# Sine stage of a two-layer transformer kernel: ScalarE writes the whole turns, VectorE makes the sine's argument from PSUM

## What is computed

```python
x = x + ffn(layernorm(x), W1, b1, theta, w_real, w_imag, W2, b2)
# ffn:
hidden = x @ W1 + b1                       # 256 -> 1024
imag   = w_imag * sin(theta + hidden * 0.1)
phase  = cos(theta) * w_real + sin(theta) * w_imag
act    = relu(hidden + phase * imag * 0.1)
out    = act @ W2 + b2                     # 1024 -> 256
```

## Time and profile before

| what | value |
|---|---|
| three runs | 991.68, 993.87, 995.29 us |
| median | 993.87 us |
| the profiled execution | 987.04 us |
| its span, first to last instruction | 985.2 us |
| granted TensorE clock, mean over the span | 0.986 of full |
| sine stage in the span | about 256 to 474.5 us |

### The profile page before, as it was taken

The page is one execution under the profiler, slowest core; times in us unless marked ns, Lnnn a source line. Parts: engine busy times, 40 slices in busy tenths (PEclk is TensorE's granted clock), DMA queues, the critical chain, the costliest instruction groups (busy, mean ns, idle before and its releaser), DMA issues. The chain is left out here.

```text
span 985.2 us, 20329 instructions
## 1 busy us (share of the span) xinstructions
PE 912.7 (93%) x7332; PEld 806.9 (82%) x7332; DVE 830.7 (84%) x2172; ACT 485.3 (49%) x1019; POOL 465.8 (47%) x663
## 2 busy tenths in 40 slices
PE   6999999999589999999799999999987999999996
PEld 4889998898478888888689889898876888888885
DVE  5799999997499999998588888899868889889874
ACT  2453443433188787788244333343454444544442
POOL 2233334331266666664322332433247777777662
PEclk9799999999799999999999999999999999999999
DMA  9020000000000000000100000000000000000000
GB/s 341 34 98 2 2 2 1 2 3 1 1 1 1 1 1 1 1 1 1 53 2 2 2 2 2 1 2 2 1 1 1 22 23 1 22 23 22 23 22 22
DMA packets 6083, 18.32 MB, mean 19 GB/s; under 512 B 864, under 2 KB 2784, under 8 KB 5472
## 3 DMA queue, kind: packets, MB, share of 16 engines
q1 hardware_dynamic: 5264, 16.52, 4.4%
q10 hardware_dynamic: 720, 0.50, 0.2%
HBM read 12.83 MB, written 4.19 MB: 17 GB/s over the span
## 5 line engine op out<-in xcount | busy, mean ns | idle before, releaser
L868 PE MATMUL a_psO<-vblk,a_prob 128*128 128x51 f32 (+1 forms) x1280 | 150.0, 273 | 0.0
L868 PEld LDWEIGHTS a_psO<-vblk,a_prob 128*128 128x128 f32 x1280 | 149.6, 194 | 0.0
L1513 PE MATMUL f_psGU<-wgu,f_xTs 128*128 128x512 f32 (+1 forms) x576 | 138.5, 385 | 3.1 <-ACT f_silu L1463 3.1
L507 DVE TENSOR_REDUCE a_mx<-a_psS 128x4 f32<-128x308 f32 x256 | 115.1, 470 | 17.4 <-PE a_psS L784 15.8
L704 ACT COPY a_xTs<-a_psQ 128x256 f32<-128x256 f32 x64 | 23.8, 372 | 206.8 <-PE a_psQ L793 206.8
L715 ACT ACTIVATE a_prob<-a_psT 128x512 f32<-128x512 f32 (+1 forms) x192 | 101.0, 526 | 40.8 <-PE a_psT L840 39.3
L1513 PEld LDWEIGHTS f_psGU<-wgu,f_xTs 128*128 128x128 f32 x576 | 101.9, 189 | 17.7 <-DVE f_xTs L1258 3.4
L840 PE MATMUL a_psT<-ident,a_shifted 128*128 128x128 f32 x640 | 106.3, 281 | 10.8 <-ACT a_prob L715 7.9
L515 DVE TENSOR_TENSOR a_shifted<-a_psS,a_mx 128x308 f32<-128x308 f32 x256 | 114.6, 469 | 0.0
L1095 PEld LDWEIGHTS s_psY<-w,s_hid 128*128 128x128 f32 x768 | 99.4, 188 | 16.6 <-POOL s_hid L1013 12.2
L1095 PE MATMUL s_psY<-w,s_hid 128*128 128x256 f32 x768 | 104.0, 284 | 5.6 <-POOL s_hid L1013 4.9
(11 more groups left out here) (157 smaller groups left out, 1912.8 us busy)
## 6 DMA issues: line engine op xcount, KB each, us to landing
out_x<-x SPq DMA_DIRECT2D x8, 512.0 KB, 2.6
x<-in_x SPq DMA_DIRECT2D x3, 1024.0 KB, 12.8
w<-in_w SPq DMA_DIRECT2D x1, 2304.0 KB, 9.1
w<-in_w SPq DMA_DIRECT2D x2, 1024.0 KB, 17.6
a_mask<-in_mask SPq DMA_DIRECT2D x4, 308.0 KB, 4.0
wat<-in_att SPq DMA_DIRECT2D x1, 1024.0 KB, 22.4
x<-in_x SPq DMA_DIRECT2D x1, 768.0 KB, 9.5
wat<-in_att SPq DMA_DIRECT2D x2, 256.0 KB, 5.5
```

Of the source, the lines that this page charges most:

```text
L507: nc.vector.tensor_reduce(mx[:, u, j * BH:(j + 1) * BH], psS[j][:, 0:BH * KV].rearrange("p (h k) -> p h k", k=KV), AX.X, ALU.max).then_inc ...
L868: mm = nc.tensor.matmul(psO[:, CH[c] * VW:(CH[c] + n) * VW], prob[:, v, c * P:(c + 1) * P], vblk[:, t // R, c * NJ * VW:(c * NJ + n) * VW] ...
L1513: mm = nc.tensor.matmul(psGU[:, n0:n1], xTs[:, u, a, k * P:(k + 1) * P], wgu[:, b, k, n0:n1], start=(n == 0), stop=(n == len(TERMS) - 1))
```

## The change

ScalarE's pass over PSUM now writes the rounded number of turns: the output tile `turn` is int32, so the conversion rounds. VectorE then makes the argument in one `scalar_tensor_tensor` (psH + phase - turns) that reads psH from PSUM and the turns from SBUF, in place of two instructions. For this, psH must already be in turns: the first weight matrix is multiplied by TURNS = 0.1 / 2 pi when it is split, the coefficient is scaled likewise, and the two Relu passes scale back. `turn` has four buffers and `arg` two. The waits follow; `turn_set` falls away.

```diff
--- before.py
+++ after.py
@@ -37,6 +37,7 @@
 MAGIC = 1.5 * 2.0 ** 23
 TWO_PI = 6.283185307179586
 PI_IN = 3.1415925
+TURNS = 0.1 / TWO_PI
 MASKED = -1e20
 
 ATT_FIRST, ATT_LAST, ATT_LOOP_FROM, ATT_LOOP_TO = -3, T + 2, 5, T - 3
@@ -335,7 +336,7 @@
         self.link(dve, nc.vector.tensor_tensor(cs, ang[:, 3, 8:16], cols[:, C_WR:C_WR + 8], ALU.mult))
         self.link(dve, nc.vector.tensor_tensor(sn, ang[:, 3, 0:8], cols[:, C_WI:C_WI + 8], ALU.mult))
         self.link(dve, nc.vector.tensor_tensor(sn, sn, cs, ALU.add))
-        self.link(dve, nc.vector.scalar_tensor_tensor(self.g["coef"][:], sn, 0.1, cols[:, C_WI:C_WI + 8], ALU.mult,
+        self.link(dve, nc.vector.scalar_tensor_tensor(self.g["coef"][:], sn, 0.1 * TURNS, cols[:, C_WI:C_WI + 8], ALU.mult,
                                                       ALU.mult))
         self.link(dve, nc.vector.tensor_scalar(thb[:], thb[:], 1.0 / TWO_PI, None, ALU.mult))
 
@@ -344,14 +345,21 @@
 
     src, high, _ = w_quarter(g, n)
     act.wait_ge(g["in_ffn"], 32)
-    nc.scalar.copy(high, src).then_inc(g["w_high"], 1)
+    if n < 2:
+        nc.scalar.activation(high, src, ACT.Copy, scale=TURNS).then_inc(g["w_high"], 1)
+    else:
+        nc.scalar.copy(high, src).then_inc(g["w_high"], 1)
 
 
 def w_low_parts(nc, dve, g, n):
 
     src, high, low = w_quarter(g, n)
     dve.wait_ge(g["w_high"], n + 1)
-    nc.vector.tensor_tensor(low, src, high.bitcast(F32), ALU.subtract).then_inc(g["w_split"], 1)
+    if n < 2:
+        nc.vector.scalar_tensor_tensor(low, src, TURNS, high.bitcast(F32), ALU.mult, ALU.subtract
+                                       ).then_inc(g["w_split"], 1)
+    else:
+        nc.vector.tensor_tensor(low, src, high.bitcast(F32), ALU.subtract).then_inc(g["w_split"], 1)
 
 
 def w_quarter(g, n):
@@ -922,8 +930,8 @@
         xTs = sb("xTs", [P, 2, 2, KC, N], F32R)
         pre = sb("pre", [P, 2, N])
         hid = sb("hid", [P, 4, 2, N], F32R)
-        arg = sb("arg", [P, 4, N])
-        turn = sb("turn", [P, 2, N])
+        turn = sb("turn", [P, 4, N], I32)
+        arg = sb("arg", [P, 2, N])
         sine = sb("sine", [P, 2, N])
 
         old_w = g["wat"][0][:].rearrange("p k n -> p (k n)")
@@ -935,8 +943,8 @@
 
         st_set, mv_ready, ve_set, rstd_ready, xhat_ready, bias_added, xT_mm, xT_high, xT_low = (sm(n) for n in (
             "st_set", "mv_ready", "ve_set", "rstd_ready", "xhat_ready", "bias_added", "xT_mm", "xT_high", "xT_low"))
-        h_mm, arg_ready, turn_set, red_ready, sine_ready, pre_ready, hid_full, hid_low, hid_used, x_done = (
-            sm(n) for n in ("h_mm", "arg_ready", "turn_set", "red_ready", "sine_ready", "pre_ready", "hid_full",
+        h_mm, turn_ready, arg_ready, sine_ready, pre_ready, hid_full, hid_low, hid_used, x_done = (
+            sm(n) for n in ("h_mm", "turn_ready", "arg_ready", "sine_ready", "pre_ready", "hid_full",
                             "hid_low", "hid_used", "x_done"))
         FIRST, LAST, LOOP_FROM, LOOP_TO = -2, NG + 1, 2, NG - 2
 
@@ -982,11 +990,11 @@
                         if valid(s2, NG):
 
                             n = NF * s2 + f2
-                            wait(dve, arg_ready, n + 1)
-                            a, k = arg[:, f2 % 4, :], turn[:, f2 % 2, :]
-                            nc.vector.tensor_scalar(k, a, MAGIC, MAGIC, ALU.add, ALU.subtract).then_inc(turn_set, 1)
-                            wait(dve, turn_set, n + 1)
-                            nc.vector.tensor_tensor(a, a, k, ALU.subtract).then_inc(red_ready, 1)
+                            wait(dve, turn_ready, n + 1)
+                            wait(dve, sine_ready, n - 1)
+                            nc.vector.scalar_tensor_tensor(arg[:, f2 % 2, :], psH[f2 % 4][:], thb[:, f2:f2 + 1],
+                                                           turn[:, f2 % 4, :], ALU.add, ALU.subtract
+                                                           ).then_inc(arg_ready, 1)
                         if f == 2 and valid(s + 1, NG):
 
                             for k in range(KC):
@@ -1036,9 +1044,9 @@
                         s1, f1 = at(s, f + 1)
                         if valid(s1, NG):
                             n = NF * s1 + f1
-                            wait(act, red_ready, n + 1)
+                            wait(act, arg_ready, n + 1)
                             wait(act, pre_ready, n - 1)
-                            nc.scalar.activation(sine[:, f1 % 2, :], arg[:, f1 % 4, :], ACT.Sin, scale=2.0 * PI_IN
+                            nc.scalar.activation(sine[:, f1 % 2, :], arg[:, f1 % 2, :], ACT.Sin, scale=2.0 * PI_IN
                                                  ).then_inc(sine_ready, 1)
                         if valid(s, NG):
                             n = NF * s + f
@@ -1046,8 +1054,10 @@
                             wait(act, hid_used, n - 3)
                             wait(act, hid_low, n - 1)
                             b1 = cols[:, C_B1 + f:C_B1 + f + 1]
-                            nc.scalar.activation(hid[:, f % 4, 0, :], pre[:, f % 2, :], ACT.Relu, bias=b1)
-                            nc.scalar.activation(full[:, f % 2, :], pre[:, f % 2, :], ACT.Relu, bias=b1
+                            nc.scalar.activation(hid[:, f % 4, 0, :], pre[:, f % 2, :], ACT.Relu, bias=b1,
+                                                 scale=1.0 / TURNS)
+                            nc.scalar.activation(full[:, f % 2, :], pre[:, f % 2, :], ACT.Relu, bias=b1,
+                                                 scale=1.0 / TURNS
                                                  ).then_inc(hid_full, 1)
                         if f == 2 and valid(s + 1, NG):
 
@@ -1059,9 +1069,9 @@
                         if valid(s2, NG):
                             n = NF * s2 + f2
                             wait(act, h_mm, n + 1)
-                            wait(act, sine_ready, n - 3)
-                            nc.scalar.activation(arg[:, f2 % 4, :], psH[f2 % 4][:], ACT.Identity,
-                                                 bias=thb[:, f2:f2 + 1], scale=0.1 / TWO_PI).then_inc(arg_ready, 1)
+                            wait(act, arg_ready, n - 3)
+                            nc.scalar.activation(turn[:, f2 % 4, :], psH[f2 % 4][:], ACT.Identity,
+                                                 bias=thb[:, f2:f2 + 1]).then_inc(turn_ready, 1)
 
                 run_steps(step, FIRST, LAST, LOOP_FROM)
```

## The result

The changed kernel takes 978.67 us (median of four runs, 976.48 to 981.67) against 993.64 us for the kernel before (four runs, 991.68 to 995.29). The two medians are 15.0 us apart. The estimated ratio of the two kernels is 0.9863, with a 95% interval of 0.9835 to 0.9891. As a gain that is 13.6 us, within 10.8 and 16.4. The forecast was 981.3 us, a gain of 12.6. Two later comparisons gave 0.9837 (0.9808 to 0.9866) and 0.9884 (0.9842 to 0.9927); their medians differ by 14.7 and 12.2 us.

A forecast was written before the change was run, and what follows sets the result against it. TensorE was taken to set the pace, delayed by a VectorE-GpSimd loop. Gains of 6 x (0.99 + 1.0) = 11.9 plus 0.7 made 12.6 us, from 993.87 to 981.3 us; range 978.5 to 989.

The forecast's parts named there:

- What bounds the kernel: Sine stage: TensorE sets the pace but waits at some places for a chain through VectorE and GpSimd; six groups lose 12.65 us.
- The three gaps: At each group boundary, two output products and the transposes come late by 0.50, 0.49 and 1.11 us, together 2.10 us.
- The loop between VectorE and GpSimd: Second half of a group: subtraction, turns, argument, aggregate, reciprocal root hold each other; VectorE's step is 3.34 us against TensorE's 2.84.
- The new argument: VectorE's argument pass, reading PSUM and int32 turns, was to take 0.74 us, within bounds of 0.69 and 1.20.
- ScalarE's write: ScalarE's pass with int32 output was to stay at 0.69 us, within bounds of 0.53 and 1.38.
- Weight splits: Scaled copies and three-operand subtractions before 54 us: at most 0.05 us each, 0.1 us as upper end, taken as nothing.
- The transposes: Group boundary: transposes could load at 4.45 us and lose 0 to 0.7, taken as 0.1; 1.0 of 1.11 us comes back.
- The ends of the stage: First output product was to gain 0.4 us and the drain of the last blocks 0.3 us, together 0.7 us.
- Carrying the profiled execution over to the median: The profiled execution was 6.83 us under the median of three runs; this difference was kept, giving 993.87 - 12.6 = 981.3 us.
- The aggregate was indeed still waited for: Rival, 12%: aggregate stays late behind the argument, waits for `hid` stay, only the transposes gain: 6.7 us, 987.2 us.
- The lock did move to the normalise: Rival, 12%: normalise meets GpSimd's subtraction in each step with one, making the step 3.13 us: gain 3.9, 990.0 us.
- ScalarE did not become the bound: Rival, 6%: a turns write of 1.38 us makes ScalarE the bound, a group needing 26.1 us: slower, 997.2 us.

The follow-up runs named there:

- e1: Changed kernel plus one VectorE pass per block ahead of the argument, psH from PSUM into a spare tile: 986.6 us, ratio 0.9933, group spacing 24.27 us.
- e2: Changed kernel plus one VectorE pass per block ahead of the argument, turns tile from SBUF into a spare tile: 987.7 us, ratio 0.9948, group spacing 24.93 us.
- e5: Kernel before, with VectorE's aggregate moved ahead of the turns and argument passes, both kept: 990.3 us, ratio 0.999, group spacing 25.17 us.
- e9: Kernel before, with only the last normalise of a group moved ahead of the residual: 995.3 us, ratio 1.0049, group spacing 26.36 us.

## Why the prediction was right

- *What bounds the kernel.* Right, to the place. The three gaps that were named made up the 12.65 us, and 12.57 of them are gone.
- *The loop between VectorE and GpSimd.* Right, by e1, e2 and e5: a pass of the removed kind costs twice what a longer one costs that has no SBUF input, and with the aggregate ahead of the passes the waits for `hid` go while both passes stay. What the sum treats as two separate losses, 0.99 for `hid` and 1.11 at the transposes, isn't separate, by e5 and e9. The addition came out because the change relieved both places at once.
- *The new argument, 0.74 us.* Measured 0.751 in the median. *ScalarE's write, 0.69.* Measured 0.690. *Weight splits at nothing.* Measured 1.062 and 1.194, against medians of 1.053 and 1.194 in the kernel before: 0.01 us for each copy. No row had shown the 0.05 that was put as its upper end.
- *The transposes.* The working was nearly exact. The trace after shows it, from the loads of block 7's product at 344.91 on:

```profile
345.06 1.29 POOL L1021 TENSOR_TENSOR s_hid<-wat,s_hid 128x512 fp32r<-128x512 f32 x1
346.31 0.73 POOL L1035 TENSOR_TENSOR x<-x,rows 128x256 f32<-128x256 f32 x1
346.78 1.29 DVE L963 TENSOR_TENSOR x<-x,s_psY 128x512 f32<-128x512 f32 x2 [1.71 <-PE s_psY L1105]
347.85 1.30 POOL L1021 TENSOR_TENSOR s_hid<-wat,s_hid 128x512 fp32r<-128x512 f32 x1 [0.81 <-ACT wat L1059]
347.99 0.74 DVE L995 SCALAR_TENSOR_TENSOR s_arg<-s_psH,thb,s_turn 128x512 f32<-128x512 f32 x1
348.65 0.65 DVE L969 TENSOR_SCALAR wat<-x,s_mv,s_rstd 128x256 f32<-128x256 f32 x1
349.36 0.87 PEld L1115 LDWEIGHTS s_psX<-ident,wat 128*128 128x128 f32 x8
```

The residual starts after 1.87 us (2.06 in the working), the argument after 3.08 (3.25), the normalise after 3.74 (3.91). The subtraction starts after 2.94 (2.9 to 3.6) and ends at 4.24, the normalise 0.15 behind it at 4.39. The transposes start at 4.45, the time at which the rhythm lets them. The normalise did meet the subtraction (0.65 and not 0.38), but with 0.06 us to spare. The 0.1 that the working charged for each boundary was the one term too many there: 0.6 us over six. That the transposes came in time was close: e1 shows that one pass more in front costs 0.68 at once.
- *The ends of the stage.* The first output product, counted from the first transposes, comes 0.74 us earlier (277.13 - 261.46 against 277.53 - 261.12), where 0.4 was taken. GpSimd's first instructions also no longer meet a turns pass: the first subtraction takes 1.27 us (1.48 before), a reciprocal root 0.55 (0.76). The clock is partly at half in this stretch, so the gain there varies between executions by some 0.4 us. The end gives 0.36, where 0.3 was taken. Together 13.7 us, where the sum had 12.6.
- *Carrying the profiled execution over to the median.* This was the weak step. The prediction took the 6.83 us between the profile of before and its median as fixed. They were the luck of one execution, its clock of 0.986. For the changed kernel's profile the step gives 974.4 us, where 977.99 was measured, and that profile lies only 0.7 under its median. The gain came out near because the sum was made almost wholly from stretches at full clock, and not because of that step.
- *The number itself.* The mechanism was right, the closeness of the total less so. The median of 978.67 lies 0.2 us above the lower end of the stated range, 978.5 to 989. In later runs of the changed kernel it was 977.16 and 978.84, the first of them just outside. Against the 13.7 us of the stage the sum was low by about 1 us: 0.6 at the transposes, 0.3 at the start of the stage, 0.1 at its end.
- *Rivals.* The aggregate was indeed still waited for (0.70 us), but the step stayed at 2.84. The lock did move to the normalise, once in a group and not in each step, as the argument against that rival had it. The Trainium skill, page "SBUF — State Buffer", section "Who interferes with whom", has the instruction that comes second blocked for all of the other's duration; the trace agrees, the normalise here ended 0.15 us after the subtraction. ScalarE did not become the bound. It has about 23.59 - 19.6 = 4.0 us left in a group, more than the prediction's 3.0.

What was not tried: a ScalarE write to int32 of other sizes; the kernel before with only its argument, or with both of its passes, made free of GpSimd.

## What to carry to other kernels

Read the pace of the bounding engine from the timeline and list the gaps that are longer than its own work. They are worth more than busy shares: here 12.57 of the stage's 13.7 us were in three gaps that recur in every group of eight blocks. When such a gap ends on another engine, look at what stands behind the slow instruction in its queue. Two moved lines gave back 1.77 of 2.10 us, but one of them alone moved the loss to another place (25.17), and the other alone made the kernel slower (26.36). And take the clock of a single profile into account before carrying its difference to a median over.

## What was not expected of the hardware

- A VectorE pass without SBUF input (0.69 us) disturbs less than one from SBUF that is shorter when free (0.41): spacing +0.68 against +1.34 us. The latter waits out GpSimd's two-input instruction: 1.20 us beside the subtraction, up to 1.55.
- int32 as an output of ScalarE and as one input of a VectorE instruction that also reads PSUM cost next to nothing: 0.690 us, as for fp32, and 0.751, where the same form with fp32 took 0.741.
- The part after the stage, the same instructions in both kernels, takes 510.1 to 515.9 us in the five profiles of the two kernels, at mean clocks between 0.974 and 0.986. That is nearly half of what this change is worth.
